# Two-layer transformer with soft and top-8 expert layers: another period table for layer 1, and the late wait written first

## Chip, cores and metric
One core of one Trainium2 chip runs the whole program. The metric is the time of one execution on the device, in microseconds (us); less is better. A program on one core has one span, and the engines named below are those of that core: PE (TensorE, matrix products), DVE (VectorE), ACT (ScalarE), POOL (GpSimd), SP (SyncE, which here issues most DMAs).

## Reference, cut to what matters
The input is 16 batches of 512 tokens with 128 features, f32. Each layer adds an attention and an expert network to the residual. Layer 0 normalizes, runs an attention with 16 heads of 8 and a rotary part, and a soft mixture of 8 experts with 64 slots each. Layer 1, in which most of the change lies, is:

```python
def _L1_attn_ref(x, w_kv_down, w_kv_up, w_q, w_out):
...
    latent_kv = x @ w_kv_down
    kv = latent_kv @ w_kv_up
    k, v = (kv[..., :HD], kv[..., HD:])
...
    att = jnp.einsum('bqhd,bkhd->bhqk', q, k) * scale
...
    att = jnp.where(causal, att, -jnp.inf)
    att = jax.nn.softmax(att, axis=-1)
    y = jnp.einsum('bhqk,bkhd->bqhd', att, v)
    y = y.reshape(Bx, Tx, HD)
    return y @ w_out

def _L1_ffn_ref(x, gate_w, expert_bias, w_gate, w_up, w_down, shared_gate_w, shared_up_w, shared_down_w):
...
    scores = jax.nn.sigmoid(gates.astype(jnp.float32))
    sel_scores = scores + expert_bias
    _, inds = jax.lax.top_k(sel_scores, K)
...
    selected = selected / selected.sum(axis=-1, keepdims=True)
    selected = selected * ROUTE_SCALE
...
    hg = jnp.einsum('bsd,eid->bsei', x, w_gate)
    hu = jnp.einsum('bsd,eid->bsei', x, w_up)
    h = jax.nn.silu(hg) * hu
    ye = jnp.einsum('bsei,edi->bsed', h, w_down)
    y = jnp.einsum('bsed,bse->bsd', ye, combine).astype(x.dtype)
    g = jnp.einsum('bsd,id->bsi', x, shared_gate_w)
    u = jnp.einsum('bsd,id->bsi', x, shared_up_w)
    y = y + jnp.einsum('bsi,di->bsd', jax.nn.silu(g) * u, shared_down_w)
    return y
...
xn = _layernorm(x, axis=-1)
x = x + _L0_attn_ref(xn, ...) + _L0_ffn_ref(xn, ...)
xn = _layernorm(x, axis=-1)
x = x + _L1_attn_ref(xn, ...) + _L1_ffn_ref(xn, ...)
```

There are 16 heads of 64 in layer 1, and K = 8 of E = 16 experts with 128 hidden values each are chosen for a token.

## The kernel before, in words
Layer 0 runs over all 16 batches, then layer 1. All 16 experts and the shared one are computed for every token; what the router did not choose gets weight 0.

**Products in halves.** A factor in f32 is split into a high and a low part in f16. A product is three matmuls into one PSUM bank: high x high, high x low, low x high (`split_product`, L1592 to L1594). So each intermediate leaves its bank twice: ACT writes the high part (q_hi, k_hi, v, lat_p and others, about L1318 to L1345), then DVE the low part (`low_part`, L1420: bank times a scale, less the high part), and after that the bank is free.

**Steps and the period table.** A batch of layer 1 is cut into steps: "load", "norm", "scale", "xnT" (normalize, transpose), "gate", "route", "cT" (router, weights, their transpose), "lat" (latent of keys and values), "qk" (per head group of 4 heads: two products of q, two of k), "v" (8 products), "max" (per head group five units of scores, whose row maxima DVE reduces in L1509 and L1513), "turn_max" (transpose of the maxima), "exp" (per pair of heads, 8 pairs, five units of scores; ACT takes their exponential twice, POOL makes the low part), "values" and "sums" (per pair: probabilities by v, and their row sums), "rec" (reciprocals of the sums of four pairs, L1525), "rec_out" and "rec_in" (these by DMA to DRAM and back, spread over the partitions), "divide" (L1533, two halves of 256 columns), "out" (the output product of four pairs, twice a batch), "gate_in" and "up_in" (two products per expert), "spread_in" (the routing weights of two experts from DRAM to all partitions, 512 KB), "hw" (the expert's hidden values in halves, L1358 and L1550), "down" (four chunks of experts, L1740), "outT", "res" (transpose, add the residual, store).

The table `ORDER1` (L953) lists the 195 steps of one period with the batch each belongs to, as an offset: ("divide", -1, 4) is pair 4 of the batch before. The program is this table repeated with the batch number counted up, from two batches before the first to two after the last, without what has no batch. Layer 0 has its own table, `ORDER0`. Every engine walks through the same list of steps and issues its own part of each, in that order, so the table fixes the order of the instructions on PE, ACT, DVE, POOL and SP alike. Nothing is reordered later: an instruction that waits holds all behind it on its engine. SP issues the DMAs of "load", "qk" (q and k stacked in SBUF), "turn_max" (the row of maxima into l_q_b), "cT" (weights to DRAM), "spread_in", "rec_out", "rec_in" and "res".

**Banks.** Layer 1 has four PSUM banks `ps_any` for everything but three things: the scores of "exp" have two banks `ps_exp`, "values" has `ps_out`, "sums" `ps_sum`. The class `Banks` (L107) walks through the table once and gives each product the bank of the four that was filled longest ago. Before its first matmul PE waits until the bank's last product was emptied (`bank`, which calls `emptied`), and a reader waits until its bank was filled (`full`, which calls `filling`). The probabilities have two slots of pairs, `p_in` three slots of units, `hid` five and `hw` eight slots of experts, `spread` three.

**Waits.** `eng.wait_ge(semaphore, count)` is put on the next instruction of the engine. An instruction carries one wait: where several are written ahead of it, the one written first stays on it, and the others become instructions of their own ahead of it.

**Shape of the array.** A matmul is named with rows x columns of the part of the array it uses: 128\*128 for products, 66\*128 for the second half of "exp", 64\*128 for "max", 128\*64 for "values", 128\*32 for "sums", 128\*16 for "turn_max".

## Time and profile before

| what | value |
|---|---|
| time, median of 3 runs | 2973.04 us (2971.9 to 2975.1) |
| the profiled execution's own time | 2973.48 us |
| its span | 2971.8 us |
| mean granted clock of PE | 0.989 of full speed |
| busy PE / DVE / ACT / POOL | 2792.8 / 2399.3 / 2074.8 / 1542.5 us |
| DMA | 298.15 MB, mean 100 GB/s |

The span goes from the first to the last instruction of the profiled execution; the rest of its own time lies around it. Matmuls overlap, and a matmul's row gives a duration in which the next one has already begun, so the distance between two starts says how long PE needs for one. A row of the timeline that ends in brackets gives the idle time of the engine ahead of it and what ended that. The granted clock is a share of 2.4 GHz. Layer 0 fills the first 1,150 us or so, layer 1 the rest.

### The profile page before, as it was taken

Reading aid. Unit: us, or ns where it says so; the run is one execution under the profiler, and the core shown is the slowest. Engines: PE = TensorE matmul, PEld = TensorE weight load, DVE = VectorE, ACT = ScalarE, POOL = GpSimd, SP = SyncE. Lnnn points to the kernel's source line nnn. Section 1 sums busy time; section 2 is a strip of 40 time slices with the busy share of each in tenths; the row PEclk is TensorE's granted clock in tenths of the full one; section 3 lists DMA queues with packets and bytes.
Section 4 is the critical chain, followed back from the end, with each engine's and each line's share of the span. In section 5 each row is a group of like instructions: output and inputs, shape, how many; then the busy total and the mean of one; then the engine's idle time right before and its main releaser. Section 6 shows DMA issues by size and latency. Waiting matters only on the chain.

```text
span 2971.8 us, 71998 instructions
## 1 busy us (share of the span) xinstructions
PE 2792.8 (94%) x27076; PEld 1596.6 (54%) x27076; DVE 2399.3 (81%) x4452; ACT 2074.8 (70%) x4411; POOL 1542.5 (52%) x1355
## 2 busy tenths in 40 slices
PE   5999999999999996999999999999999999999998
PEld 2555555555555553555555555555555555555554
DVE  6777777777777776888888888888888888888886
ACT  3777777677677765777777777777777777777764
POOL 2333333333333333665666666666666666666664
PEclk8999999999999998999999999999999999999999
DMA  4222222222222224454454464464454454454452
GB/s 126 59 55 55 66 67 56 68 58 57 55 58 61 55 55 128 109 142 113 115 145 118 110 148 115 111 150 113 111 149 113 112 149 112 112 146 115 111 147 69
DMA packets 272089, 298.15 MB, mean 100 GB/s; under 512 B 30848, under 2 KB 235648, under 8 KB 271488
## 3 DMA queue, kind: packets, MB, share of 16 engines
q1 hardware_dynamic: 247424, 274.70, 37.0%
q10 hardware_dynamic: 24320, 18.85, 2.0%
q8 instruction: 217, 3.56, 0.5%
q14 instruction: 128, 1.05, 0.1%
HBM read 141.39 MB, written 25.69 MB: 56 GB/s over the span
## 4 chain that ended last, share of the span: by engine, by line
PE 48%; DVE 6%; issue 3%; ACT 2%; DMA 1%; POOL 1%; SPq 0%; ACTq 0%; DVEq 0%; POOLq 0%
PE l_ps_out L1703 7%; PE l_ps_any L1592 5%; PE l_ps_any L1593 5%; PE l_ps_any L1594 5%; PE l_ps_exp L1684 4%; PE l_ps_any L1740 4%; PE l_ps_exp L1686 4%; PE l_ps_any L1749 4%; PE l_ps_any L1659 3%; PE l_ps_sum L1725 2%; PE l_ps_exp L1688 2%; PE l_ps_any L1664 1%; PE l_ps_any L1586 1%; DVE l_yT L1533 1%; DVE l_select L1431 1%
## 5 line engine op out<-in xcount | busy, mean ns | idle before, releaser
L1268 POOL TENSOR_TENSOR stage<-l_p_in,stage 128x512 f16<-128x512 f32 x640 | 759.3, 1198 | 405.5 <-ACT l_p_in L1381 404.5
L695 DVE TENSOR_REDUCE neg_max<-ps_any 128x1 f32<-128x384 f32 (+3 forms) x704 | 413.2, 635 | 118.3 <-PE ps_any L824 117.9
L1377 ACT ACTIVATE stage<-l_ps_exp 128x512 f16<-128x512 f32 x640 | 388.2, 607 | 157.3 <-PE l_ps_exp L1688 135.9
L1277 POOL TENSOR_TENSOR l_hid<-l_hid,l_spread 128x512 f32<-128x512 f32 x256 | 340.8, 1336 | 247.4 <-DVE l_hid L1546 211.8
L555 ACT ACTIVATE probs<-ps_exp 128x512 f32<-128x512 f32 x640 | 348.0, 605 | 95.4 <-PE ps_exp L839 90.6
L469 POOL TENSOR_SCALAR_AFFINE_SELECT probs<-probs 128x512 f32<-128x512 f32 x256 | 165.4, 664 | 441.6 <-ACT probs L555 441.6
L1381 ACT ACTIVATE l_p_in<-l_ps_exp 128x512 f32<-128x512 f32 x640 | 390.3, 610 | 0.0
L1513 DVE TENSOR_REDUCE l_neg_max<-l_ps_any 128x2 f32<-128x768 f32 (+2 forms) x384 | 310.9, 863 | 17.0 <-PE l_ps_any L1664 13.9
L822 PE MATMUL ps_any<-k_st,q_st 120*128 120x128 f16 (+3 forms) x1024 | 255.6, 305 | 70.8 <-DMA k_st<-stack_scratch 43.8
L1684 PE MATMUL l_ps_exp<-l_q_a,l_k_a 128*128 128x512 f16 (+3 forms) x1024 | 304.8, 300 | 3.2 <-DMA l_q_b<-l_max_row 1.6
L1686 PE MATMUL l_ps_exp<-l_q_b,l_k_b 66*128 66x512 f16 (+3 forms) x1024 | 295.5, 300 | 0.0
L1550 DVE TENSOR_TENSOR l_hw<-l_hid,l_hw 128x512 f16<-128x512 f32 x272 | 239.6, 886 | 6.2 <-ACT l_hw L1358 4.6
L1703 PE MATMUL l_ps_out<-stage,l_v 128*64 128x512 f16 (+3 forms) x3072 | 233.1, 301 | 0.0
L1387 ACT ACTIVATE l_hid<-l_ps_any 128x512 f32<-128x512 f32 x272 | 160.7, 614 | 102.8 <-PE l_ps_any L1594 98.2
L839 PE MATMUL ps_exp<-q_st,k_st 121*128 121x512 f16 (+3 forms) x1024 | 218.1, 302 | 4.6 <-DMA q_st<-max_row 2.4
L1688 PE MATMUL l_ps_exp<-l_mask_h,l_ident_h 128*128 128x128 bf16 x1024 | 212.5, 219 | 0.0
L1740 PE MATMUL l_ps_any<-l_hw,l_w_d 128*128 128x512 f16 x816 | 186.7, 379 | 16.3 <-DVE l_q_lo L1420 16.3
L824 PE MATMUL ps_any<-mask_h,ident_h 128*128 128x128 bf16 x1024 | 200.2, 221 | 0.0
L1358 ACT ACTIVATE l_hw<-l_hid 128x512 f16<-128x512 f32 x272 | 173.0, 642 | 33.3 <-POOL l_hid L1277 30.3
L1540 DVE SCALAR_TENSOR_TENSOR l_hid<-l_hid,l_ps_any 128x512 f32<-128x512 f32 x272 | 178.4, 678 | 21.2 <-ACT l_hid L1387 20.9
L1703 PEld LDWEIGHTS l_ps_out<-stage,l_v 128*64 128x64 f16 x3072 | 154.2, 110 | 76.1 <-issue 11.2
L459 POOL TENSOR_SCALAR disp_s<-disp_s,c_rec 128x512 f32<-128x512 f32 x64 | 105.4, 1652 | 167.7 <-DVE c_rec L704 167.7
(262 smaller groups left out, 6739.1 us busy)
## 6 DMA issues: line engine op xcount, KB each, us to landing
l_spread<-route_scratch SPq DMA_DIRECT2D x128, 512.0 KB, 5.0
l_q_a<-l_q_hi SPq DMA_DIRECT2D x256, 128.0 KB, 2.4
l_y_rec<-rec_scratch SPq DMA_DIRECT2D x128, 256.0 KB, 4.6
l_q_b<-l_q_lo SPq DMA_DIRECT2D x128, 128.0 KB, 2.4
l_k_a<-l_k_hi SPq DMA_DIRECT2D x128, 128.0 KB, 2.6
l_k_a<-l_k_lo SPq DMA_DIRECT2D x128, 128.0 KB, 2.8
l_k_b<-l_k_hi SPq DMA_DIRECT2D x128, 128.0 KB, 2.7
q_st<-rot_hi SPq DMA_DIRECT2D x64, 128.0 KB
```

What stands on the lines that cost most here:

```text
L555: nc.scalar.activation(probs[:, n % 2, u], ps_exp[:, (10 * g + u) % 3], ACT.Exp, scale=float(HD0 + DR) ** -0.5).then_inc(exp_done.sem, 1)
L695: nc.vector.tensor_reduce(neg_max[:, n % 2, heads[0]:heads[0] + k, t], src, AX.X, ALU.max, negate=True).then_inc(drained["dve"], 1)
L1268: nc.gpsimd.tensor_tensor(probs[:, n % 2, 1, u], p_in[:, m % P_SLOTS], probs[:, n % 2, 0, u], ALU.subtract).then_inc(p_lo_ok.sem, 1)
L1277: nc.gpsimd.tensor_tensor(at, at, spread[:, c % 3, n % SPREAD], ALU.mult).then_inc(weighted.sem, 1)
L1377: nc.scalar.activation(probs[:, n % 2, 0, u], bank, ACT.Exp, scale=float(HD1) ** -0.5).then_inc(exp_done.sem, 1)
L1381: nc.scalar.activation(p_in[:, m % P_SLOTS], bank, ACT.Exp, scale=float(HD1) ** -0.5).then_inc(p_ok.sem, 1)
L1513: ins = nc.vector.tensor_reduce(maxima[:, :, q, t], scores[:, :, c:c + (t + 1) * P], AX.X, ALU.max, negate=True)
L1684: pe.matmul(out, k_a[:, g % 2, h, k * P:k * P + P], q_a[:, g % 2, h, k * P:T], start=True, stop=False)
L1686: pe.matmul(out, k_b[0:K_B, g % 2, h, k * P:k * P + P], q_b[0:K_B, g % 2, h, k * P:T], start=False, stop=False)
L1688: ins = pe.matmul(out[:, 0:P], ident_h[:], mask_h[:], start=False, stop=True)
L1703: ins = pe.matmul(ps_out[HD1 * r:HD1 * r + HD1, k * P:T], v[:, k, cv, h * HD1:h * HD1 + HD1], probs[:, n % 2, cp, u, c:c + T - k * P], sta ...
L1740: ins = pe.matmul(out, w_d[:, cw, e], hw[:, k % HW_SLOTS, cx], start=(e == todo[0] and cw + cx == 0), stop=(e == todo[-1] and cw == 1))
```

## The change
Two things are changed.

1. The table `ORDER1` is another one. It has the same steps of each kind per period; "load" stands one batch further ahead (offset 2), and some steps of the next batch have come into the table of the period, others of the batch before have left it. `ORDER0` stays.
2. Where several waits are written ahead of an instruction, their order is changed. In "exp" ACT waits first for the scores, then for "values" and "sums" of the pair before. `low_part` (DVE) waits first for the high part, and for its bank not at all, since the high part's ACT instruction has waited for that; so do "slots", "low_q", "low_k", "dispatch", "combine" and one "logits" of layer 0. "hidden" of layer 0 waits first for its bank. "values" and "sums" (PE) wait first for the low parts of the probabilities. "logits" of layer 0 waits for xfT for n = 0 alone.

Two lines are added in layer 1 and one in layer 0, so L1420 before is L1423 now, L1533 is L1536, L1592 is L1595, L1740 is L1743. The diff, with the table cut to its first lines:

```diff
@@ exp of layer 1, ACT (the same in layer 0, there with pv_done alone)
                     p, u = PAIRS * b + n, step[3]
+                    act.wait_ge(exp_full.sem, exp_full.at(p, u + 1))
                     if u == 0 and p >= 2:
                         act.wait_ge(pv_done.sem, pv_done.at(p - 1, 0))
                         act.wait_ge(summed.sem, summed.at(p - 1, 0))
-                    act.wait_ge(exp_full.sem, exp_full.at(p, u + 1))
@@ low_part of layer 1, DVE
-                bank = full(dve, name)
                 dve.wait_ge(sem.sem, count)
+                bank = ps_any[:, banks.at[name]]
@@ slots of layer 0, DVE (so too dispatch, combine, low_q, low_k; logits on ACT)
-                    bank = full(dve, f"slots{b}")
+                    bank = ps_any[:, banks.at[f"slots{b}"]]
                     dve.wait_ge(slots_hi.sem, slots_hi.at(b, 1))
@@ hidden of layer 0, ACT
+                    bank = full(act, f"hidden{b}_{n}")
                     if b and n == 0:
                         filling(act, f"expert_out{b - 1}")
-                    bank = full(act, f"hidden{b}_{n}")
@@ logits_s and logits_c of layer 0, PE
-                    emptied(pe, f"xfT{b}")
+                    if n == 0:
+                        emptied(pe, f"xfT{b}")
@@ values of layer 1, PE
                     p = PAIRS * b + n
+                    pe.wait_ge(p_lo_ok.sem, p_lo_ok.at(p, 5))
                     if p:
                         pe.wait_ge(y_ok.sem, y_ok.at(p, 0))
                     if n % SET == 0:
                         emptied(pe, f"v{b}_{TB - 1}{n // SET}")
-                    pe.wait_ge(p_lo_ok.sem, p_lo_ok.at(p, 5))
@@ sums of layer 1, PE
+                    pe.wait_ge(p_lo_ok.sem, p_lo_ok.at(p, 5))
                     if j == 0 and p >= SET:
                         pe.wait_ge(rec_ok.sem, rec_ok.at(p // SET, 0))
-                    pe.wait_ge(p_lo_ok.sem, p_lo_ok.at(p, 5))
@@ the table
 ORDER1 = (
-    ("max", 0, 0, 2), ("max", 0, 0, 3), ("values", -1, 5), ("max", 0, 0, 4), ("divide", -1, 1), ("hw", -1, 15),
...
+    ("exp", -1, 7, 2), ("qk", 0, 1, 0), ("exp", -1, 7, 3), ("outT", -2), ("rec_in", -1, 1), ("gate_in", 0, 1),
...
```

What the table moves is shown at three places, in a batch in the middle of layer 1.

**First place, PE, "down" of chunk 0.** Before, it stands behind one gate product, one k product and a unit of "exp", all behind the two q products of head group 2 (w_q is q's weight, w_kvu that of keys and values, w_g the experts' gate weight):

```order
L1592 MATMUL l_ps_any<-l_xn_p,l_w_g 128x512 [waits l1_drained_dve]
L1593 MATMUL l_ps_any<-l_xn_p,l_w_g 128x512
L1594 MATMUL l_ps_any<-l_xn_p,l_w_g 128x512
L1592 MATMUL l_ps_any<-l_lat_p,l_w_kvu 128x512 [waits l1_drained_dve]
L1593 MATMUL l_ps_any<-l_lat_p,l_w_kvu 128x512
L1594 MATMUL l_ps_any<-l_lat_p,l_w_kvu 128x512
L1684 MATMUL l_ps_exp<-l_q_a,l_k_a 128x512 [waits l1_p_ok]
L1686 MATMUL l_ps_exp<-l_q_b,l_k_b 128x512
L1688 MATMUL l_ps_exp<-l_mask_h,l_ident_h 128x128
L1740 MATMUL l_ps_any<-l_hw,l_w_d 128x512 [waits l1_hw_ok,l1_drained_dve]
L1740 MATMUL l_ps_any<-l_hw,l_w_d 128x512 x2
```

Now, in the same batch, after the last units of "exp" of a pair:

```order
L1687 MATMUL l_ps_exp<-l_q_a,l_k_a 128x256
L1689 MATMUL l_ps_exp<-l_q_b,l_k_b 128x256
L1691 MATMUL l_ps_exp<-l_mask_h,l_ident_h 128x128
L1595 MATMUL l_ps_any<-l_xn_p,l_w_g 128x512 [waits l1_drained_dve]
L1596 MATMUL l_ps_any<-l_xn_p,l_w_g 128x512
L1597 MATMUL l_ps_any<-l_xn_p,l_w_g 128x512
L1743 MATMUL l_ps_any<-l_hw,l_w_d 128x512 [waits l1_hw_ok,l1_drained_dve]
L1743 MATMUL l_ps_any<-l_hw,l_w_d 128x512 x2
...
L1595 MATMUL l_ps_any<-l_xn_p,l_w_q 128x512 [waits l1_drained_dve]
L1596 MATMUL l_ps_any<-l_xn_p,l_w_q 128x512
L1597 MATMUL l_ps_any<-l_xn_p,l_w_q 128x512
```

"down" has moved ahead of the q and k products of head group 2; a gate product alone stands between it and "exp", and the first q product comes after it.

**Second place, DVE, "divide" of pairs 4 and 5 of the batch before** (two rows each, l_yT<-l_yT,l_y_rec). Before, each stands between low parts of q and k of head group 2:

```order
L1420 SCALAR_TENSOR_TENSOR l_v<-l_ps_any,l_v 128x512 [waits l1_v_hi_ok,l1_filled]
L1533 TENSOR_TENSOR l_yT<-l_yT,l_y_rec 128x2x128 [waits l1_rec_in,l1_y_ok]
L1533 TENSOR_TENSOR l_yT<-l_yT,l_y_rec 128x256
L1420 SCALAR_TENSOR_TENSOR l_q_lo<-l_ps_any,l_q_hi 128x512 [waits l1_hi_ok,l1_filled]
L1550 TENSOR_TENSOR l_hw<-l_hid,l_hw 128x512 [waits l1_hw_hi]
L1533 TENSOR_TENSOR l_yT<-l_yT,l_y_rec 128x2x128 [waits l1_rec_in,l1_y_ok]
L1533 TENSOR_TENSOR l_yT<-l_yT,l_y_rec 128x256
L1420 SCALAR_TENSOR_TENSOR l_k_lo<-l_ps_any,l_k_hi 128x512 [waits l1_hi_ok,l1_filled]
L1540 SCALAR_TENSOR_TENSOR l_hid<-l_hid,l_ps_any 128x512 [waits l1_filled,l1_tanh_ok]
L1420 SCALAR_TENSOR_TENSOR l_k_lo<-l_ps_any,l_k_hi 128x512 [waits l1_hi_ok,l1_filled]
L1550 TENSOR_TENSOR l_hw<-l_hid,l_hw 128x512 [waits l1_hw_hi]
L1557 TENSOR_SCALAR l_acc<-l_ps_any 128x512 [waits l1_filled]
```

Now (the first "divide" here is that of pair 3):

```order
L1536 TENSOR_TENSOR l_yT<-l_yT,l_y_rec 128x2x128 [waits l1_rec_in,l1_y_ok]
L1536 TENSOR_TENSOR l_yT<-l_yT,l_y_rec 128x256
L1549 TENSOR_TENSOR l_hid<-l_ps_any,l_hid 128x512 [waits l1_filled,l1_drained_dve] x2
L1564 SCALAR_TENSOR_TENSOR l_acc<-l_ps_any,l_acc 128x512 [waits l1_drained_dve,l1_filled]
L1512 TENSOR_REDUCE l_neg_max<-l_ps_any 128x2x2 [waits l1_filled]
L1516 TENSOR_REDUCE l_neg_max<-l_ps_any 128x2 [waits l1_filled]
L1516 TENSOR_REDUCE l_neg_max<-l_ps_any 128x2
L1536 TENSOR_TENSOR l_yT<-l_yT,l_y_rec 128x2x128 [waits l1_rec_in,l1_y_ok]
L1536 TENSOR_TENSOR l_yT<-l_yT,l_y_rec 128x256
L1553 TENSOR_TENSOR l_hw<-l_hid,l_hw 128x512 [waits l1_hw_hi]
L1536 TENSOR_TENSOR l_yT<-l_yT,l_y_rec 128x2x128 [waits l1_rec_in,l1_y_ok]
```

All three have come close together, ahead of the first low part of head group 2, with two reductions of "max" (L1512, L1516) and an add to the accumulator (L1564) between pair 3 and pair 4.

**Third place, PE, the transpose of the maxima of the next batch's head group 0** (L1669 before, L1672 now). Before, units of "exp" of the pair before follow it:

```order
L1725 MATMUL l_ps_sum<-stage,l_ones_in 32x256 x2
L1725 MATMUL l_ps_sum<-stage,l_ones_in 32x128 x6
L1669 MATMUL l_ps_any<-ident,l_neg_max 16x128 [waits l1_drained_dve]
L1684 MATMUL l_ps_exp<-l_q_a,l_k_a 128x384 [waits l1_p_ok]
L1686 MATMUL l_ps_exp<-l_q_b,l_k_b 128x384
L1688 MATMUL l_ps_exp<-l_mask_h,l_ident_h 128x128
L1684 MATMUL l_ps_exp<-l_q_a,l_k_a 128x128
```

Now six products follow, and then the first "exp" that reads the row of maxima (it waits for l1_row_in):

```order
L1672 MATMUL l_ps_any<-ident,l_neg_max 16x128 [waits l1_drained_dve]
L1595 MATMUL l_ps_any<-l_xn_p,l_w_q 128x512 [waits l1_drained_dve]
L1596 MATMUL l_ps_any<-l_xn_p,l_w_q 128x512
...
L1595 MATMUL l_ps_any<-l_lat_p,l_w_kvu 128x512 [waits l1_drained_dve]
L1596 MATMUL l_ps_any<-l_lat_p,l_w_kvu 128x512
...
L1595 MATMUL l_ps_any<-l_xn_p,l_w_u 128x512 [waits l1_drained_dve]
...
L1595 MATMUL l_ps_any<-l_xn_p,l_w_u 128x512 [waits l1_drained_act]
...
L1595 MATMUL l_ps_any<-l_lat_p,l_w_kvu 128x512 [waits l1_drained_dve]
...
L1595 MATMUL l_ps_any<-l_xn_p,l_w_g 128x512 [waits l1_drained_dve]
...
L1687 MATMUL l_ps_exp<-l_q_a,l_k_a 128x512 [waits l1_p_ok,l1_stacked,l1_row_in]
```

Before, twelve products and the rest of the exp units stood between the two; now it is six products alone.

## Rows read from the trace of the kernel before

**Rows 1.** The page, part 1: busy time, share of the span, instructions
```profile
PE 2792.8 (94%) x27076; PEld 1596.6 (54%) x27076; DVE 2399.3 (81%) x4452; ACT 2074.8 (70%) x4411; POOL 1542.5 (52%) x1355
```
**Rows 2.** Window of one period: us, PE, PEld, DVE, ACT, POOL busy, PEclk, DMA, GB/s
```profile
1650.20:1761.20 111.00, 109.28 (x1074) 60.91 (x1072) 96.50 (x162) 80.12 (x159) 70.41 (x58) 1.00 0.52 125
```
**Rows 3.** Instructions of L1557: ns min/median/max, first and last start
```profile
L1557 DVE TENSOR_SCALAR l_acc<-l_ps_any x16: 676/678/692, 1215.7 to 2882.4; 128x512 f32<-128x512 f32 x16
```
**Rows 4.** Waits of PE, 1300 to 2850: us in total, times, longest us
```profile
PE l_ps_any L1740 <- DVE l_q_lo L1420: 15.5, 14, 1.5
PE l_ps_any L1592 <- DVE l_lat_p L1420: 5.3, 14, 0.4
PE l_ps_exp L1684 <- DMA l_q_b<-l_max_row: 1.6, 3, 0.8
```
**Rows 5.** Timeline, PE, 2000 to 2012: start us, us, engine, line, operation, count
```profile
2003.04 0.22 PE L1688 MATMUL l_ps_exp<-l_mask_h,l_ident_h 128*128 128x128 bf16 x1
2003.10 0.38 PE L1592 MATMUL l_ps_any<-l_xn_p,l_w_u 128*128 128x512 f16 x1
...
2010.73 0.22 PE L1688 MATMUL l_ps_exp<-l_mask_h,l_ident_h 128*128 128x128 bf16 x1
2010.88 1.33 PE L1703 MATMUL l_ps_out<-stage,l_v 128*64 128x512 f16 x12
```
**Rows 6.** Timeline, PE: round two transposes of maxima and a k product
```profile
1756.33 0.28 PE L1669 MATMUL l_ps_any<-ident,l_neg_max 128*16 128x128 f32 x1
...
1760.89 0.38 PE L1684 MATMUL l_ps_exp<-l_q_a,l_k_a 128*128 128x512 f16 x1
...
2006.77 0.38 PE L1594 MATMUL l_ps_any<-l_lat_p,l_w_kvu 128*128 128x512 f16 x1
```
**Rows 7.** Timeline, ACT and DVE, 2004 to 2008: high and low parts
```profile
2004.67 0.60 ACT L1336 ACTIVATE l_q_hi<-l_ps_any 128x512 f16<-128x512 f32 x1 [0.29 <-PE l_ps_any L1594]
2005.37 0.69 DVE L1420 SCALAR_TENSOR_TENSOR l_q_lo<-l_ps_any,l_q_hi 128x512 f16<-128x512 f32 x1 [0.67 <-ACT l_q_hi L1336]
...
2007.19 0.60 ACT L1336 ACTIVATE l_k_hi<-l_ps_any 128x512 f16<-128x512 f32 x1
```
**Rows 8.** Tile slotsT, layer 0, 150 to 1070: who waited for it, us, times
```profile
  PEld ps_any L763: 4.9, 13
```
**Rows 9.** Timeline, DVE and PE, 1762 to 1767: "divide" and "down"
```profile
1762.13 2.41 DVE L1533 TENSOR_TENSOR l_yT<-l_yT,l_y_rec 128x256 f32<-128x256 f32 x2
...
1763.76 0.22 PE L1688 MATMUL l_ps_exp<-l_mask_h,l_ident_h 128*128 128x128 bf16 x1
1765.19 1.04 PE L1740 MATMUL l_ps_any<-l_hw,l_w_d 128*128 128x512 f16 x4 [1.22 <-DVE l_q_lo L1420]
...
1766.02 0.75 DVE L1533 TENSOR_TENSOR l_yT<-l_yT,l_y_rec 128x256 f32<-128x256 f32 x2
```
**Rows 10.** Timeline, DVE: first instruction of "route" and the one behind it
```profile
1698.08 0.21 DVE L1429 TENSOR_SCALAR l_score<-l_th 128x64 f32<-128x64 f32 x1
...
1703.41 0.68 DVE L1420 SCALAR_TENSOR_TENSOR l_q_lo<-l_ps_any,l_q_hi 128x512 f16<-128x512 f32 x1
```
**Rows 11.** DMA issues, 1300 to 2850: count, KB each, median us to landing
```profile
l_spread<-route_scratch SPq DMA_DIRECT2D x111, 512.0 KB, 5.0
...
l_y_rec<-rec_scratch SPq DMA_DIRECT2D x112, 256.0 KB, 4.6
...
l_q_b<-l_max_row SPq DMA_DIRECT2D x56, 4.0 KB, 3.0
route_scratch<-l_weightT SPq DMA_DIRECT2D x14, 32.0 KB, 1.9
```
**Rows 12.** Timeline, POOL, 1717 to 1736: the batch's first weighting
```profile
1727.90 1.27 POOL L1277 TENSOR_TENSOR l_hid<-l_hid,l_spread 128x512 f32<-128x512 f32 x1 [2.79 <-DMA l_spread<-route_scratch]
```
**Rows 13.** Groups by line, 1500 to 2700: busy us, mean ns, idle before
```profile
L1550 DVE TENSOR_TENSOR l_hw<-l_hid,l_hw 128x512 f16<-128x512 f32 x183 | 159.6, 877 | 1.2
L1533 DVE TENSOR_TENSOR l_yT<-l_yT,l_y_rec 128x256 f32<-128x256 f32 x172 | 90.2, 565 | 0.6 <-DMA l_y_rec<-rec_scratch 0.6
```

76 lines of the change are left out of this document (39 added, 37 removed).

## Prediction

> **What bounds the kernel now.** I read the page first: PE is busy for 94% of the span, DVE 81%, ACT 70%, POOL 52% [rows 1]. Then one period of layer 1 (one batch), the part whose order changes: PE works 109.28 of 111.00 us, DVE 96.50 beside it, at a granted clock of 1.00 [rows 2]. The first "down" of a batch starts the accumulator, from 1215.7 to 2882.4 us over 16 batches: (2882.4 - 1215.7) / 15 = 111.11 us a period [rows 3]. So PE is the bound, and time can go in two ways: less work on PE, or shorter waits of PE. The list of waits shows what PE stood still for in 14 periods: 15.5 us (1.11 a period) before "down" for l_q_lo on DVE, 5.3 us (0.38) before a product for l_lat_p, 1.6 us before exp for a DMA [rows 4]. Idle is counted from the end of the last matmul; start to start a wait costs 0.16 us more, since a matmul of 0.22 us is followed by the next after 0.06 us [rows 5]. The two big waits thus cost 1.27 and 0.54, together 1.8 us a period.
>
> **Changes of the array's shape.** After an exp's last 128-column matmul (128*128) the next one starts 0.06 us later if it has the same shape (2003.04, 2003.10), but 0.15 us later if it is the 128*64 of "values" (2010.73, 2010.88) [rows 5]. A change costs 0.09 us. Counted in the table ("max" is 64*128, "values" 128*64, "sums" 128*32, all else full width), a period has 49 changes before and 44 after; the whole program, its ends included, 782 and 703. The 79 that go are worth 79 x 0.093 = 7.3 us (0.08 and 0.10 by the rounding: 6 to 8), all on PE; nothing hides them.
> The Trainium skill, "TensorEngine Tiling (Array Packing)", Key Properties, says that changing the tiling mode drains the engine, and "TensorE: Matmul & The Clock Gate", Part 2, puts the drain at about 128 cycles; by these pages 79 changes would be an estimated 4.2 us at 2.4 GHz, and the sum 3 us higher. The rows have 0.09 for one, and I take them.
>
> **Waits written in another order.** The first wait that is written rides on the instruction, the others become instructions of their own ahead of it. ACT's l_k_hi, which waits for its bank alone, starts at 2007.19, as its matmul ends (2006.77 + 0.38 = 2007.15): 0.04 us. On DVE l_q_lo, whose late wait was written second, starts at 2005.37, 0.10 us after its l_q_hi (2004.67 + 0.60) [rows 6, 7]. So 0.06 us or a little more a time, where the wait was really late. In layer 1 this touches the first exp of a pair and DVE's low parts; PE's two big waits there end on a DVE queue that was busy before the job, so the cover is that queue, and without it the price is at most two such jobs, 0.1 us a period. I take nothing. In layer 0 one such place is on PE's way: PE waited for DVE's slotsT 13 times in 13 batches [rows 8], and the first "hidden" behind it has its bank wait moved to the front too. That is 16 x 2 x 0.06 = 1.9 us. Layer 0's order and banks stay. The repeated waits that go (a low part's bank, which the high part has waited for; xfT for n > 0) lie in queues that run ahead: nothing, and nothing to lose. On PE, "values" and "sums" now carry the wait for the low parts and check the others first, which are long met.
>
> **The waits that the new order removes.** "down" of chunk 0 takes the bank of the second q product of head group 2. DVE's queue shows why it is late: two halves of "divide" take 2.41 us (1762.13), l_q_lo stands behind them, and PE, which waits for it, starts at 1765.19 where it would have started 0.06 us after 1763.76 [rows 9]. In the new order (the first place shown) "down" stands before these products and takes a bank of "max", left 2.15 us of PE's work earlier, with one reduction of 1.2 us to wait for. The 1.27 us go. The second wait comes from "route", 5.33 us of DVE in one piece (1698.08 to 1703.41) [rows 10], behind which lat's low part stood; now lat stands before it. Behind route now stand two k products; the first of their banks is wanted again 3.05 us of PE's work later, about when DVE has it free: 0 to 0.5 us, I take 0.1. Net 1.7 us a period.
>
> **What is late next.** Four places are tighter; PE's work between steps is counted from the order at 0.65 us a product of three matmuls (four of "down" take 1.04 us [rows 9], one 0.38, so 0.22 from start to start).
> (a) The row of maxima of head group 0: transpose, ACT, a DMA of SP (median 3.0 us [rows 11]), exp. Now six products lie between, 6 x 0.65 + 0.11 = 4.0 us (third place), where there were 12. Head group 1 has 1756.33 to 1760.89, 4.56 us [rows 6], and the only waits of this kind, 1.6 us in 14 periods [rows 4]. With 0.56 us less: 0.4 us a period (0 to 1.5).
> (b) POOL's first weighting of a batch waits for the spread table; it already idles 2.79 us for it, to 1727.90, with no harm [rows 12]. From cT: 1.1 us to the end of ACT's copy, 1.9 to DRAM, 5.0 back [rows 11], 1.27 for the weighting and three low parts at 1.2, 12.9 us, until "sums" of pair 7 has what it needs; PE gets there after 15.4. With two spreads and a load in flight the landing grows: 0.2 us (0 to 1.2).
> (c) After the fourth unit of "max" of head group 3 DVE has two reductions (2.4), two reciprocals (1.8), three jobs and a v low part (3.0), 7.2 us, and that v's bank is wanted 7.1 us after DVE could begin: 0.4 us (0 to 1.5).
> (d) "divide" of pairs 4 and 5 follows that of pair 3 after 8 us of PE's work instead of 18 (second place). Between them lies the trip of the reciprocals, two issues by SP and 4.6 us to landing [rows 11]: 0.3 us (0 to 2).
> Together 1.3 us, with 0.1 for the rest of the ring 1.4 against 1.7 removed: 0.3 x 16 = 5 us.
>
> **Sum.** -7.3 - 1.9 - 5 = -14 us against the profiled execution's 2973.5 us (span 2971.8), which lies 0.4 us above the median of the runs, 2973.0. Start and tail have the same steps, the tail the same trips of the reciprocals: nothing, 3 us either way. **2959 us.** Bounds: every new wait at zero gives -7.3 - 1.9 - 29 = 2935. The upper ends add to 6.2 us a period, but a wait at one place gives the queues time at the next; half of it, 3.1 against 1.8, gives -9 + 21, 2985.
>
> **Rivals.**
> A. The new order has next to no waits. For it: DVE has 14.5 us free in a period. Against: (a), (c) and (d) are each at the edge. -9 - 27: 2937 us. Chance 0.21.
> B. The waits come back in full size elsewhere. The change then doesn't do what a new order is for, since DVE has 96.5 us of work in 111 and four banks to hand over, whatever the order [rows 2]; the shapes remain, less what is added: 2970 us (2964 to 2976). Chance 0.14.
> C. Slower, by (d). If the reciprocals land later than DVE arrives, DVE stands still with all behind it, and the add of "out", four jobs on, holds the bank that the next "max" wants 1.3 us after "out": each us of lateness is one of PE, 16 in all. For it: I put DVE at divide 4 some 14 us into the period, and the landing at 13.3 to 15. Against: "out" itself is 3.4 us of PE's work and covers the first of it. From 2.3 us of new waits a period it is slower than before; at 3.3 it is 2989 us. Chance 0.21.
> D. DVE's jobs with two operands in SBUF meet POOL's more often. l_hw has a mean of 877 ns and a half of divide 565 [rows 13], where l_q_lo has 680 for as many columns and an undisturbed half 0.37 [rows 9]: 17 x 0.2 + 16 x 0.2 = 6.6 us a period already. The new order sets hw and divide in groups; 2 us more of it would give PE perhaps 0.8: 2972 us. Chance 0.06.
> The Trainium skill, "SBUF — State Buffer", on the shared port pair, says that such an operation and a GpSimd one that reads SBUF exclude each other for the whole instruction.
>
> **How the numbers follow.** The forecast's own case (2949 to 2967) has 0.38. A measurement can tell about 0.2%, 6 us. Faster by more: 0.38 + 0.21 + 0.06 of B = 0.65. Within: 0.08 of B + 0.06 of D = 0.14. Slower: C, 0.21. The range goes from A's low end, 2935, to 2988, and leaves out half of C and a little of A.
>
> **What would show it.** A period of 110.2 us between first "down"s; L1740's idle for l_q_lo and L1592's for l_lat_p gone; PE's wait for max_row before exp under 0.5 us a period, and for POOL before "sums" under 0.4. It is wrong if PE's idle before "max" for l_acc, or DVE's before l_yT for a DMA, passes 1 us a period, if the first low part of v becomes a wait of over 1 us, or if layer 0's period moves by more than 0.3 us.

## The result and the profile after

The changed kernel takes 2979.15 us (median of 16 runs, 2972.46 to 2985.15), the kernel before 2972.38 us (16 runs, 2970.78 to 2975.10). The ratio is 1.0024 with an interval of 1.0016 to 1.0032: 0.24% slower, some 7 us, where 14 us faster was forecast. The runs of the changed kernel also lie further apart, 12.7 us against 4.3.

That small number is the sum of two large ones. The page's first part and the two steps that occur once in a batch show them. First the busy times, which answer to [rows 1]:

```profile
PE 2792.6 (94%) x27076; PEld 1599.7 (54%) x27076; DVE 2451.9 (82%) x4452; ACT 2075.0 (70%) x4411; POOL 1583.8 (53%) x1355
```

PE has as much to do as before; DVE is busy 52.6 us longer with the same 4452 instructions. Now one instruction of layer 0 (ACT's slotsT, L540 before, L541 after) and the first "down" of layer 1 (L1560, before in [rows 3]): duration in ns, then first and last start. Of before:

```profile
L540 ACT ACTIVATE slotsT<-ps_any x16: 597/597/598, 74.1 to 1100.9; 128x512 f16<-128x512 f32 x16
```

and of after:

```profile
L541 ACT ACTIVATE slotsT<-ps_any x16: 597/597/597, 72.8 to 1084.4; 128x512 f16<-128x512 f32 x16
L1560 DVE TENSOR_SCALAR l_acc<-l_ps_any x16: 677/678/679, 1187.7 to 2887.4; 128x512 f32<-128x512 f32 x16
```

By (last - first start) / 15, layer 0 went from 68.45 to 67.44 us a batch, though its table is the same, and layer 1 from 111.11 to 113.31. The last slotsT comes 16.5 us earlier, "down" runs through its 15 periods in 1699.7 us instead of 1666.7, 33 us more.

What PE waited for in layer 1, 1300 to 2850 us, the same view as [rows 4] (us in total, times, longest us):

```profile
PE l_ps_any L1595 <- DVE l_v L1423: 23.1, 27, 1.3
PE l_ps_any L1662 <- DVE l_acc L1569: 22.2, 13, 2.0
PE l_ps_any L1752 <- DVE l_yT L1536: 4.2, 14, 0.3
PE l_ps_any L1595 <- DVE l_acc L1560: 1.0, 3, 0.3
PE l_ps_any L1662 <- DVE l_neg_max L1512: 0.2, 1, 0.2
```

The two waits of before, for l_q_lo and l_lat_p, are gone, as the change means it. In their place stand two others, for l_v and for l_acc, and together they are twice as long: 50.7 us of idle in 58 waits against 23.9 in 35. With the 0.16 us that each wait costs from start to start beyond its idle time, that is (50.7 + 9.3) / 14 = 4.3 us a batch against 2.1.

### Where layer 1's new wait comes from

The list of DVE's waits of the changed kernel begins with a DMA, of which the kernel before has 0.6 us in all between 1500 and 2700 [rows 13]:

```profile
DVE l_yT L1536 <- DMA l_y_rec<-rec_scratch: 47.3, 16, 4.3
```

One batch of it, on DVE: the reciprocals, "divide" of pair 3 and "divide" of pair 4 (start us, us):

```profile
2062.10 1.76 DVE L1528 RECIPROCAL l_rec<-l_ps_sum 128x128 f32<-128x128 f32 x2
...
2067.31 2.11 DVE L1536 TENSOR_TENSOR l_yT<-l_yT,l_y_rec 128x256 f32<-128x256 f32 x2
...
2077.71 0.91 DVE L1536 TENSOR_TENSOR l_yT<-l_yT,l_y_rec 128x256 f32<-128x256 f32 x2 [3.85 <-DMA l_y_rec<-rec_scratch]
```

The DMA queue of SP in the same stretch:

```profile
2061.59 0.53 SPq L1221 DMA_DIRECT2D l_spread<-route_scratch  x1
2062.16 0.59 SPq L1201 DMA_DIRECT2D l_k_a<-l_k_hi  x1
...
2065.44 0.61 SPq L1201 DMA_DIRECT2D l_k_b<-l_k_hi  x1
2066.16 0.52 SPq L1221 DMA_DIRECT2D l_spread<-route_scratch  x1
2066.80 0.38 SPq L1229 DMA_DIRECT2D rec_scratch<-l_rec  x1
2071.85 9.30 SPq L1238 DMA_DIRECT2D l_y_rec<-rec_scratch  x4
```

And PE, which stands still for the add of "out" behind "divide":

```profile
2081.24 0.34 PE L1662 MATMUL l_ps_any<-l_k_hi,l_q_hi 64*128 64x384 f16 x2 [1.74 <-DVE l_acc L1569]
2081.46 0.23 PE L1662 MATMUL l_ps_any<-l_k_hi,l_q_hi 64*128 64x128 f16 x2
2081.68 1.82 PE L1706 MATMUL l_ps_out<-stage,l_v 128*64 128x512 f16 x24
```

The reciprocals are ready at 2063.86. SP is then in the middle of six stack DMAs of k and a spread of 512 KB, so rec_out goes out at 2066.80, 2.9 us late (median of such places 3.3 us; before 0.1). It lands 5.0 us later (median 4.7; before 1.7), 0.36 us after the spread that was issued 0.64 us ahead of it. So it is in nearly every batch: in the changed kernel a spread is under way at 31 of the 32 issues of rec_out, and 30 of these land 0.3 to 0.5 us after the spread does; in the kernel before none of the 32 meets a spread. rec_in follows at 2071.85 and lands at about 2077.6. DVE has stood still since 2073.9. This is the mechanism of rival C, and it is what (d) put at 0.3 us.

### The profile page after: what moved, and what is told of

Same layout as the page of the kernel before. It is cut to its first block, busy times and chain, and to the rows that moved or that the text cites. A ratio compares the mean times of both kernels' runs of the same rounds, so it can differ in the third digit from the quotient of the medians.

```text
span 2982.3 us, 71219 instructions
## 1 busy us (share of the span) xinstructions
PE 2792.6 (94%) x27076; PEld 1599.7 (54%) x27076; DVE 2451.9 (82%) x4452; ACT 2075.0 (70%) x4411; POOL 1583.8 (53%) x1355
## 4 chain that ended last, share of the span: by engine, by line
PE 32%; DVE 12%; issue 6%; DMA 6%; SPq 3%; POOL 2%; ACT 1%; ACTq 0%; POOLq 0%; DVEq 0%
PE l_ps_out L1706 5%; PE l_ps_any L1595 4%; PE l_ps_any L1743 4%; DVE l_yT L1536 4%; PE l_ps_any L1597 3%; PE l_ps_any L1596 3%; DMA l_y_rec<-rec_scratch 3%; PE l_ps_exp L1687 3%; PE l_ps_exp L1689 3%; PE l_ps_any L1662 3%; DMA rec_scratch<-l_rec 2%; SPq L1201 2%; DVE l_hw L1553 2%; PE l_ps_sum L1728 2%; DVE l_hid L1543 1%
## 5 line engine op out<-in xcount | busy, mean ns | idle before, releaser
L1271 POOL TENSOR_TENSOR stage<-l_p_in,stage 128x512 f16<-128x512 f32 x640 | 785.8, 1243 | 372.3 <-ACT l_p_in L1384 371.4
L1280 POOL TENSOR_TENSOR l_hid<-l_hid,l_spread 128x512 f32<-128x512 f32 x256 | 348.4, 1366 | 271.0 <-DVE l_hid L1549 249.2
L1516 DVE TENSOR_REDUCE l_neg_max<-l_ps_any 128x2 f32<-128x768 f32 (+2 forms) x384 | 315.1, 863 | 40.4 <-PE l_ps_any L1667 37.2
L1536 DVE TENSOR_TENSOR l_yT<-l_yT,l_y_rec 128x256 f32<-128x256 f32 x256 | 203.1, 838 | 61.7 <-DMA l_y_rec<-rec_scratch 61.4
L1553 DVE TENSOR_TENSOR l_hw<-l_hid,l_hw 128x512 f16<-128x512 f32 x272 | 245.7, 912 | 2.3 <-ACT l_hw L1361 1.9
L1549 DVE TENSOR_TENSOR l_hid<-l_ps_any,l_hid 128x512 f32<-128x512 f32 x272 | 180.9, 679 | 12.8 <-PE l_ps_any L1597 12.3
L1743 PE MATMUL l_ps_any<-l_hw,l_w_d 128*128 128x512 f16 x816 | 188.0, 382 | 0.0
```

The source lines that it names most:

```text
L1271: nc.gpsimd.tensor_tensor(probs[:, n % 2, 1, u], p_in[:, m % P_SLOTS], probs[:, n % 2, 0, u], ALU.subtract).then_inc(p_lo_ok.sem, 1)
L1280: nc.gpsimd.tensor_tensor(at, at, spread[:, c % 3, n % SPREAD], ALU.mult).then_inc(weighted.sem, 1)
L1516: ins = nc.vector.tensor_reduce(maxima[:, :, q, t], scores[:, :, c:c + (t + 1) * P], AX.X, ALU.max, negate=True)
L1536: ins = nc.vector.tensor_tensor(part, part, y_rec[:, f, n % 2].rearrange("p (c q) -> p c q", q=P), ALU.mult)
L1743: ins = pe.matmul(out, w_d[:, cw, e], hw[:, k % HW_SLOTS, cx], start=(e == todo[0] and cw + cx == 0), stop=(e == todo[-1] and cw == 1))
```

## The experiments

All runs, in the order in which they were made. The medians of e1 to e12 are of 4 to 6 executions each, and each ratio is to executions of the kernel before made along with them (medians 2969.4 to 2972.0). "Layer 0" and "layer 1" are us a batch of the profiled execution, (last - first start) / 15 of slotsT and of the first "down".

| run | what it is | median us | ratio to before (interval) | layer 0 | layer 1 |
|---|---|---|---|---|---|
| before | | 2972.4 | 1 | 68.45 | 111.11 |
| after | | 2979.2 | 1.0024 (1.0016 to 1.0032) | 67.44 | 113.31 |
| e1_waits | old table, new waits | 2947.8 | 0.9921 (0.9908 to 0.9933) | 67.25 | 110.99 |
| e2_table | new table, old waits | 3005.4 | 1.0113 (1.0099 to 1.0126) | 68.47 | 113.37 |
| e3_table_loads | before, two edits on ACT | 2946.9 | 0.9923 (0.9909 to 0.9936) | 66.93 | 111.12 |
| e4_rec_first | after, rec and rec_out earlier | 2958.3 | 0.9954 (0.9941 to 0.9966) | 67.29 | 111.73 |
| e5_spread_behind | after, a spread behind rec_out | 2961.6 | 0.9966 (0.9953 to 0.9978) | 67.17 | 111.86 |
| e6_divide_behind_v | e4, divide 6 later | 2947.4 | 0.9919 (0.9904 to 0.9933) | 66.97 | 111.21 |
| e7_divide_behind_q | e1, divide 4 later | 2946.2 | 0.9913 (0.9898 to 0.9929) | 66.95 | 110.83 |
| e8_both_new_table | e5, divide 6 later | 2953.3 | 0.9935 (0.9920 to 0.9950) | 66.88 | 111.41 |
| e9_rec_out_first | e8, rec_out alone earlier | 2951.0 | 0.9935 (0.9920 to 0.9950) | 66.95 | 111.29 |
| e10_divide_behind_hw | e9, divide 6 later still | 2939.8 | 0.9894 (0.9880 to 0.9909) | 67.11 | 110.75 |
| e11_hidden_alone | before, one of e3's edits | 2955.9 | 0.9949 (0.9932 to 0.9966) | 67.45 | 111.11 |
| e12_divide_3_earlier | e10, divide 3 earlier | 2948.5 | 0.9924 (0.9910 to 0.9937) | 66.91 | 111.31 |

### The two halves apart: e1_waits and e2_table

e1 is the changed kernel with `ORDER1` of before, e2 the kernel before with `ORDER1` of after; no other line differs.

> The table of before with every wait in its new order. Theory: in layer 0 the load of ACT's function table for Gelu (L572) and for Exp (L527) carried the bank's wait and so began only when PE was done; with the new order it begins early, and a batch of layer 0 takes 66.5 us instead of 68.15. If that is all of it, and layer 1's period stays at 111.1 us, the time is 2973 - 16 x 1.65 = 2947 us (2943 to 2955). Rival, my own prediction: waits cost 0.06 us each and the new order gives 2 us, 2971 us. If layer 1 gains or loses by the waits, its period moves from 111.1 us; I expect less than 0.2 us.

> The new table with every wait as before. Theory: the gain of the change is layer 0's waits alone and the loss is layer 1's table alone, so this one lacks the gain: layer 0 at 68.15 us a batch, layer 1 at 113.5 us, 2979 + 22 = 3001 us (2993 to 3008). Rival: the new order of waits is what slows layer 1 (values and sums wait first for the low parts, exp first for its scores): then layer 1's period falls towards 110.2 us here and the time is about 2960 us.

Measured: 2947.8 and 3005.4 us. The waits alone are worth -24 us, the table alone +33. Both together should give 2972.4 - 24.6 + 33 = 2981; it is 2979.2. The two add up to within 2 us, and the rival that the new order of waits slows layer 1 falls: layer 1 is at 113.37 us with the old waits too, and at 110.99 with the new ones on the old table.

### Why layer 0 is faster: e3_table_loads and e11_hidden_alone

The waits of PE in layer 0, 150 to 1070 us, before:

```profile
PE ps_any L822 <- ACT disp_s L527: 8.6, 14, 0.6
...
PE ps_any L828 <- ACT hT L572: 7.2, 13, 0.6
PE ps_any L822 <- ACT max_row L545: 3.4, 14, 0.2
```

All three are on ACT, and none is in the same list of after. They are 19.2 us of idle in 41 waits, 25.8 us with 0.16 us for each. ACT's timeline of one batch, before:

```profile
348.39 0.60 ACT L562 ACTIVATE y_un<-ps_out 128x512 f32<-128x512 f32 x1
350.27 1.28 ACT L572 ACT_TABLE_LOAD   x1 [1.28 <-PE ps_any L765]
351.56 3.39 ACT L572 ACTIVATE hT<-ps_any,b 128x64 f32<-128x64 f32 x16
...
359.15 1.28 ACT L527 ACT_TABLE_LOAD   x1 [0.90 <-PE ps_any L765]
360.45 0.69 ACT L527 ACTIVATE disp_s<-ps_any,c_neg 128x512 f32<-128x512 f32 x1
```

and after:

```profile
340.66 0.60 ACT L563 ACTIVATE y_un<-ps_out 128x512 f32<-128x512 f32 x1
341.27 1.28 ACT L573 ACT_TABLE_LOAD   x1
342.57 3.38 ACT L573 ACTIVATE hT<-ps_any,b 128x64 f32<-128x64 f32 x16
...
349.78 1.28 ACT L528 ACT_TABLE_LOAD   x1
351.08 0.69 ACT L528 ACTIVATE disp_s<-ps_any,c_neg 128x512 f32<-128x512 f32 x1
```

ACT changes its function table twice a batch, for Gelu and back for Exp, 1.28 us each. No line of the kernel says so; the load has the line of the activation it serves. The trace's records of ACT show what held it. The load waits for nothing itself. The activation has the wait that was written first, and the wait for the bank, written second, is an instruction of its own, which ends at 350.24 and 359.13 us. It stands ahead of the load, and the load starts right behind it, at 350.27 and 359.15. So for "hidden" ACT idled 1.28 us until PE had filled the bank, and only then loaded the table, and 0.90 us for Exp. In the changed kernel the bank's wait of "hidden" is on the activation, behind the load, and that of Exp is gone; the load runs at once, beside PE's work. e3 makes these two edits alone, on the kernel before:

```diff
                 if name in ("soft_s", "soft_c"):
-                    nc.scalar.activation(w[:, n], full(act, f"logits{name[4:]}{b}_{n}"), ACT.Exp, ...
+                    logits = ps_any[:, banks.at[f"logits{name[4:]}{b}_{n}"]]
+                    nc.scalar.activation(w[:, n], logits, ACT.Exp, ...
                 if name == "hidden":
+                    bank = full(act, f"hidden{b}_{n}")
                     if b and n == 0:
                         filling(act, f"expert_out{b - 1}")
-                    bank = full(act, f"hidden{b}_{n}")
```

> Before, with two edits in layer 0 on ACT alone: hidden waits for its bank first, and the logits' bank wait ahead of Exp goes. Theory: these two free the table loads and hold nearly all of the gain of the new waits, 1.3 to 1.7 us a batch: 2946 to 2953 us, within 5 us of all the new waits on the old table. Rival: the gain comes from the 17 wait instructions that are gone per batch on ACT and DVE; two of these would give at most an eighth of it, 2970 us.

Measured 2946.9 us, as much as all the new waits (2947.8). The groups of the two loads over the program (busy us, mean ns, idle before) are, before:

```profile
L572 ACT ACT_TABLE_LOAD x16 | 20.5, 1283 | 20.6 <-PE ps_any L765 20.6
L527 ACT ACT_TABLE_LOAD x16 | 20.5, 1283 | 14.3 <-PE ps_any L765 14.3
```

and in e3:

```profile
L573 ACT ACT_TABLE_LOAD x16 | 20.5, 1283 | 1.7 <-PE ps_any L766 1.4
L528 ACT ACT_TABLE_LOAD x16 | 20.5, 1283 | 0.3
```

The other new waits, on DVE, on PE and in layer 1, give nothing that can be told: the rival of the 17 fewer wait instructions falls. e11 takes the edit on "hidden" alone (the last three lines of the diff).

> Before, with one edit: hidden of layer 0 waits for its bank first, so that the wait no longer stands on the load of Gelu's table (1.28 us, L572). Theory: the load starts when ACT is free and PE's idle before L828 for hT (0.57 us a batch) and before L822 for max_row (0.24) goes; with the 0.16 us between end and start of matmuls counted, 0.8 to 1.0 us a batch: 2972 - 14 = 2958 us (2954 to 2962), and the other edit (the logits' bank wait on Exp's table load) has the rest, 0.6 to 0.8 us a batch. Rival: the two loads are in one chain, and freeing one alone gives either nothing (2970) or all (2948).

Measured 2955.9 us, 14 to 16 us of the 25. PE's waits for hT and max_row are gone, the one for disp_s is still 8.7 us in 14 batches. So neither load hides the other; each is worth its own waits. (Layer 0's periods of 66.9 to 67.4 us in the runs that have both edits differ for another reason, told under "Clock" below.)

### Why layer 1 is slower: e4_rec_first, e5_spread_behind, e9_rec_out_first

These runs change when rec_out goes out. In e4 the reciprocals go earlier, on DVE and SP. In e5 only the spread goes behind them. e8 is e5 with divide 6 moved (below), and e9 is e8 with rec_out alone earlier, a step of SP:

```diff
 after:  ("hw", 0, 0), ("qk", 0, 1, 3), ("gate_in", 0, 4), ("exp", 0, 0, 0), ("spread_in", 0, 3), ("rec", -1, 1), ("rec_out", -1, 1),
+e4:     ("hw", 0, 0), ("rec", -1, 1), ("rec_out", -1, 1), ("qk", 0, 1, 3), ("gate_in", 0, 4), ("exp", 0, 0, 0), ("spread_in", 0, 3),
+e5:     ("hw", 0, 0), ("qk", 0, 1, 3), ("gate_in", 0, 4), ("exp", 0, 0, 0), ("rec", -1, 1), ("rec_out", -1, 1), ("spread_in", 0, 3),
+e9:     ("hw", 0, 0), ("rec_out", -1, 1), ("qk", 0, 1, 3), ("gate_in", 0, 4), ("exp", 0, 0, 0), ("spread_in", 0, 3), ("rec", -1, 1),
```

> The changed kernel with rec and rec_out of the second half of the heads moved ahead of the last k product of head group 1, so that the reciprocals leave before SP's six stack DMAs and before the spread of 512 KB (spread_in 3 now stands behind them). Theory: DVE's idle of 2.5 to 4.3 us a batch before l_yT for l_y_rec falls below 1 us, PE's idle before max for l_acc (22 us in 14 batches) to under 0.3 us a batch, and the dips of the granted clock behind it go: 1.5 to 2.2 us a batch, 2979 - 30 = 2949 us (2942 to 2962). Rival 1: DVE is too full for it, the waits of PE move to the first low part of v or to out, and less than 0.5 us a batch is gained: 2972 us or more. Rival 2: the two reciprocals of 0.9 us that now stand earlier hold the banks of the q and k products: a new wait of PE there of over 0.5 us a batch.

> The changed kernel with one step put later: spread_in 3 (512 KB) stands behind rec and rec_out, no longer ahead of them; rec stays where it is. Theory: what made the reciprocals late was mostly the spread issued 0.6 us ahead of them (their trip to DRAM took 3.7 to 5.5 us, 1.8 in the kernel before); now rec_out goes out 0.6 us earlier and lands after 2 us, rec_in starts 3.5 us earlier, DVE's idle before l_yT falls from 3.4 us a batch to under 0.8, PE's for l_acc to under 0.3. Without the earlier reciprocals there is no new wait for l_k_lo either: layer 1 at 111.4 us a batch (111.0 to 112.0), 2950 us (2944 to 2960). Rival: it was SP's queue of six stack DMAs ahead of rec_out (2.9 us after the reciprocals' end) that counted; then the spread moves only 0.6 us and the collision is merely turned round, DVE still waits over 2 us a batch, and the time stays above 2968 us.

> The changed kernel with rec_out (a step of SP alone) moved ahead of the last k product of head group 1, so ahead of SP's six stack DMAs and of the spread; the reciprocals on DVE stay where they are, and divide of pair 6 stands behind the low part of v 2,1. Theory: the trip is late by both, issue queue (2.9 us) and collision (3.2 us); with both gone rec_out is issued 0.1 us after the reciprocals and DVE's idle for l_y_rec is under 0.3 us a batch, PE has neither the wait for l_acc nor the one for l_k_lo that the earlier reciprocals brought. Layer 1 at 110.7 us a batch (110.4 to 111.1), 2947 - 13 = 2934 us (2929 to 2942). Rival: SP, standing still for the reciprocals, brings the stack DMAs late and exp waits for them; or DVE's queue, which no longer idles, gives the wait at another bank: 2944 us or more.

For the trip of the second half's reciprocals the traces give these medians, and beside them DVE's idle for l_y_rec and PE's for l_acc between 1300 and 2850 us:

| run | reciprocals' end to rec_out's issue | issue to landing | DVE for l_y_rec | PE for l_acc (L1569) |
|---|---|---|---|---|
| before | 0.1 us | 1.7 us | under 1 us | none |
| after | 3.3 | 4.7 | 47.3 | 22.2 |
| e4_rec_first | 0.1 | 3.6 | 7.4 | 1.0 |
| e5_spread_behind | 2.6 | 3.8 | 22.8 | 9.8 |
| e9_rec_out_first | 0.1 | 2.0 | 21.0 | 11.2 |

e4 shows the theory right: with the reciprocals in time PE's wait for l_acc falls from 22.2 to 1.0 us, layer 1 gains 1.6 us a batch, and 21 us of the program go, of the 30 forecast. Its second rival came true as well, for a smaller amount: a wait of 10.0 us in 14 batches for l_k_lo, behind the reciprocals that now stand earlier on DVE. e5 falls between theory and rival (2961.6 us, forecast under 2960 or over 2968): half of DVE's idle went, with 0.7 us less lag and a landing 0.9 us faster, and half stayed. In e9 rec_out leaves at once, when the spread ahead of it has only about 1.5 us to go, and lands in 2.0 us, yet DVE still idles 21 us, and the expectation of 2934 us was missed by 17. Its SP queue says why:

```profile
2045.74 0.33 SPq L1229 DMA_DIRECT2D rec_scratch<-l_rec  x1
...
2051.25 1.24 SPq L1238 DMA_DIRECT2D l_y_rec<-rec_scratch  x2
```

rec_out had landed at 2047.7, but rec_in went out at 2051.25, 0.03 us after the end of "divide" of pair 3. There is one table l_y_rec for two pairs, and rec_in waits until the last divide has read it (`y_div` in SP's "rec_in"). So the chain is: divide 3, rec_in, 6.6 us to landing (2057.9), divide 4, and the new table leaves only six other instructions of DVE, 4.5 us, between the two divides. A second table of reciprocals should cut this chain; that was not tried. e12 moves divide 3 three jobs ahead instead (behind hw 1):

> The run with divide of pair 6 behind hw 11, and divide of pair 3 three jobs of DVE earlier, behind hw 1. There is one table of reciprocals in SBUF for two pairs, so rec_in of pairs 4 and 5 waits for the end of divide 3, whatever rec_out does: in the last two runs its DMAs were issued 0.03 us after that end and landed 5.3 to 6.5 us later, and DVE, four jobs on, idled 1.0 to 2.2 us. Theory: with divide 3 some 2 us earlier this idle falls from 1.6 to under 0.4 us a batch and PE's for l_acc from 0.85 to under 0.2; layer 1 at 110.2 us a batch, 2940 - 12 = 2928 us (2923 to 2934). Rival: divide 3, 2.1 us under POOL's work, now stands ahead of three jobs whose banks PE wants, and gives a new wait of as much there: 2936 us or more.

DVE's idle for l_y_rec fell to 3.0 us and PE's for l_acc to 0.5, as the theory has it. The time rose to 2948.5 us from e10's 2939.8, where 2928 was forecast. Its rival has come true; of PE's two largest waits the first is new:

```profile
PE l_ps_any L1595 <- DVE l_hid L1549: 19.6, 14, 1.4
PE l_ps_any L1752 <- DVE l_yT L1536: 6.9, 12, 0.6
```

### The other new wait: e6_divide_behind_v, e7_divide_behind_q, e8_both_new_table, e10_divide_behind_hw

The wait for l_v stands behind "divide" of pair 6. DVE and POOL there, in the changed kernel:

```profile
2012.23 2.81 DVE L1536 TENSOR_TENSOR l_yT<-l_yT,l_y_rec 128x256 f32<-128x256 f32 x2
2014.96 0.68 DVE L1423 SCALAR_TENSOR_TENSOR l_v<-l_ps_any,l_v 128x512 f16<-128x512 f32 x1
```

```profile
2011.79 1.66 POOL L1280 TENSOR_TENSOR l_hid<-l_hid,l_spread 128x512 f32<-128x512 f32 x1 [0.71 <-DVE l_hid L1549]
2013.40 1.34 POOL L1271 TENSOR_TENSOR stage<-l_p_in,stage 128x512 f16<-128x512 f32 x1
```

The two halves take 1.5 and 1.4 us instead of the 0.37 each of [rows 9] (0.75 us for two). They end 0.3 us after POOL's two instructions (2013.45 and 2014.74). So it is with nearly every half longer than 0.7 us: 47 of the 48 before and 115 of the 131 after (of 256 each) end 0.28 to 0.29 us after a POOL instruction does; the mean of a half between 1500 and 2700 us rose from 565 ns [rows 13] to 854:

```profile
L1536 DVE TENSOR_TENSOR l_yT<-l_yT,l_y_rec 128x256 f32<-128x256 f32 x168 | 136.0, 854 | 40.1 <-DMA l_y_rec<-rec_scratch 40.0
```

Over the whole program the 256 halves took 69.6 us more (214.6 against 145.0), which is more than DVE's extra 52.6 us; "route" and others took less. POOL's instructions took 41.3 us more in all. The Trainium skill, "SBUF — State Buffer", on the shared port pair, says that a DVE operation with both inputs in SBUF and a GpSimd operation that reads SBUF exclude each other for the whole instruction; the ends of the long halves agree with that. The runs move these divides behind the low part that PE wants, each against the run named in the table:

```diff
+e6, e8:  ("v", 0, 2, 1), ("divide", -1, 6),
-         ("divide", -1, 6), ("v", 0, 2, 1),
+e7:      ("spread_in", 0, 5), ("qk", 0, 2, 1), ("divide", -1, 4), ("hw", 0, 5),
-         ("divide", -1, 4), ("spread_in", 0, 5), ("qk", 0, 2, 1), ("hw", 0, 5),
+e10:     ("v", 0, 2, 1), ("exp", 0, 4, 2), ("gate_in", 0, 13), ("gate_in", 0, 14), ("hw", 0, 11), ("divide", -1, 6),
-         ("v", 0, 2, 1), ("divide", -1, 6), ("exp", 0, 4, 2), ("gate_in", 0, 13), ("gate_in", 0, 14), ("hw", 0, 11),
```

> The run with rec first, and beside it divide of pair 6 behind the low part of v 2,1 instead of ahead of it. Theory: that divide takes 2.8 us instead of 0.8, because POOL works at the same time, and the low part behind it is what PE waited for 1.3 us a batch before a gate product; now this wait is under 0.2 us. With 0.16 us of start to start that is 1.3 us a batch, 2958 - 20 = 2938 us (2933 to 2945). Rival: the queue of DVE stays as long, the wait comes back within the next 15 us at another bank, and less than 0.4 us a batch is gained: 2952 us or more.

> The old table with the new waits, and divide of pair 4 behind the low part of the second q product of head group 2 instead of ahead of it. Theory: PE's largest wait of the kernel before, 1.07 us of idle a batch before down for l_q_lo, is this divide at 2.4 us under POOL's work ahead of the low part; with it behind, the wait falls below 0.1 us: 1.1 to 1.2 us a batch, 2948 - 18 = 2930 us (2925 to 2937), without a new table. Rival: the k products' low parts behind the divide become late instead and half or more comes back: 2939 us or more.

> The changed kernel with spread_in 3 behind rec_out and divide of pair 6 behind the low part of v 2,1. By the theory both waits of PE go without a new one: layer 1 at 110.2 us a batch (109.9 to 110.7), what its five fewer changes of shape were worth among it; 2979 - 16 x 3.3 = 2926 us (2921 to 2938). If it does not get below the old table with the new waits (2948 us) the new table gives nothing even when its two new waits are gone.

> The run before this, and divide of pair 6 another three jobs of DVE later, behind hw 11. In the kernel with rec first and the divide behind v, 9.0 us of PE's idle for l_hid and 6.5 us for l_v in 14 batches were left. Theory: both are this divide's 2.8 us under POOL's work ahead of a low part that is wanted soon; three jobs later it stands before nothing that is wanted soon: PE's idle for l_hid and l_v together under 0.3 us a batch, 0.8 us a batch less than without this move, 2934 - 13 = 2921 us. Rival: DVE is behind by a fixed amount and the wait moves on once more: less than 0.3 us a batch, within 5 us of the run before this.

e6: 2947.4 us, 11 us gained where 20 were forecast; the 18 us of waits for the first of the two l_v went, and 9.0 us came back for l_hid behind the same divide. e7: 2946.2 us, against 2930 forecast. The largest wait of the kernel before, for l_q_lo (14.9 us in e1), is gone, and in the old table 11.4 us for l_k_lo stand in its place; nothing that can be told was gained. This is what the rivals of both runs say. e8: 2953.3 us against 2926; of the changed kernel's two waits neither went, l_v's shrank to 6.3 us and l_acc's to 12.4, and 8.9 us for l_hid are new. So it does not get below the old table with the new waits (2947.8). e10: 2939.8 us against 2921, 11 us less than e9, where its own step was forecast at 13: three jobs later the divide no longer delays l_hid, whose 9.0 us are gone. 5.4 us for l_v stay, and the wait for l_yT grew from 3.8 to 7.4. It is the fastest version of the study, 1.1% faster than before (0.9894, 0.9880 to 0.9909); some 25 of the 33 us are the table loads.

## Why the prediction was wrong, point by point

**The waits removed from layer 1** ("The 1.27 us go"; lat now 0.1): right. Neither stands in the list of after.

**Shapes** (-7.3 us): no run tested them alone, but the sums agree. e10 has the new table's 44 changes, e1 the old one's 49. e1's idle is 22.8 us in 32 waits, e10's 24.9 in 42, so with 0.16 us each 1.99 and 2.26 us a batch. 110.99 + 0.27 - 5 x 0.093 = 110.80 us; measured 110.75. The Trainium skill's drain of about 128 cycles at the end of a matmul ("TensorE: Matmul & The Clock Gate", Part 2), an estimated 0.05 us, would, if it is what a change costs, give 111.0 us instead; the sum is too coarse to rule it out.

**The order of waits in layer 0** ("16 x 2 x 0.06 = 1.9 us"): the step that was most wrong. They are worth 25 us (e1, e3). The price of 0.06 us was for a wait that becomes an instruction of its own right ahead of the work; I did not ask what stands between the two. For "hidden" and the router's Exp a table load of 1.28 us stands there. The program's lines don't show it, and the groups and the timeline of before do, with "1.28 <-PE" behind it. That layer 0's period moves by more than 0.3 us was named as a sign that the forecast is wrong, and it moved by 1.0. The other three signs came too: PE's idle for l_acc before "max" and DVE's for a DMA before l_yT passed 1 us a batch (1.6 and 3.4), and the first low part of v became a wait of 1.3 us.

**(a)** the row of maxima, 0.4 us a batch: it cost nothing, and the 1.6 us of before went with it. **(b)** the spread, 0.2: no wait at "sums" in the list of after.

**(c)** v behind the reciprocals, 0.4 us (0 to 1.5): right in place, wrong in size. The v of the second half waits 1.3 us a batch, at the upper bound with 0.16 us more from start to start, and another v adds 0.3 to 0.6. The term put three jobs and the low part of v together at 3.0 us; "divide" of pair 6, which stands right ahead of that low part, alone took 2.8 us, and e6, with it behind, has 18 us less of this wait.

**(d)** "two issues by SP and 4.6 us to landing: 0.3 us (0 to 2)": the term that gave the sign. It measured 3.4 us of DVE's idle and 1.6 us of PE's a batch, inside its bounds and over five times its value. With the reciprocals out in time (e4) 21 us of the program go, and the change would have been a gain. The trip was taken with the durations of before. In the new place rec_out waits 3.3 us in SP's queue, lands in 4.7 us instead of 1.7 beside a spread, and rec_in waits for divide 3 as well (e9, e12). Every DMA issue on the queue and every reuse of the tile should have been written down, as the place itself was.

**A term that is missing**: the wait for l_yT before "out" (L1752), 4.2 us of idle in 14 waits, 0.46 us a batch with 0.16 us for each. Before it is not in the list.

**D** (DVE against POOL): had a chance of 0.06 and 2 us of DVE's time a batch. It came beside C, and at twice its size on DVE: the halves of "divide" alone grew by 16 x 0.29 = 4.6 us a batch. What PE lost by it is shown at one place, "divide" of pair 6 (e6); elsewhere it was not separated.

**Clock**: not in the prediction. In the changed kernel's profile the granted clock falls to the lower level four times in layer 1 between 1700 and 2800 us, where before it stays at 1.00. One of these (columns as in [rows 2]), and PE there:

```profile
1737.00:1741.00 4.00, 2.26 (x25) 1.18 (x23) 4.00 (x8) 1.57 (x3) 1.10 (x2) 1.00 0.02 8
1741.00:1745.00 4.00, 4.00 (x41) 2.32 (x36) 1.36 (x3) 0.70 (x2) 0.38 (x1) 0.57 0.47 127
```

```profile
1740.55 0.34 PE L1662 MATMUL l_ps_any<-l_k_hi,l_q_hi 64*128 64x384 f16 x2 [1.74 <-DVE l_acc L1569]
1740.99 3.21 PE L1706 MATMUL l_ps_out<-stage,l_v 128*64 128x512 f16 x24
```

The same "values" took 1.82 us at 2081.68. At the lower level, 1.2 GHz for some microseconds, it loses 1.4 us, right behind the idle for l_acc. With about 1.7 us for each of four such places in 14 batches this is 0.5 us a batch, and the account of layer 1 closes: 4.28 - 2.11 = 2.2 us more waits, less 0.47 for shapes, plus 0.5, gives 2.2; measured 113.31 - 111.11 = 2.20. e2, the same table with the old waits, had no such fall and 55.8 us of idle in 68 waits, 4.76 us a batch: 4.76 - 2.11 - 0.47 = 2.18, measured 2.26. All four falls came right behind an idle of 1.7 to 2.0 us for l_acc. Why not behind the others (2081 had 1.74 us, and one of 2.02 us at 1627 had none behind it either) stays open, and no run tested it alone. Layer 0 has such falls too, in different number from run to run: between 150 and 1050 us none before, four in the changed kernel (67.44 us a batch), two in e1 and e4 (67.25, 67.29), none in e8 and e9 (66.88, 66.95). At up to 1.7 us each in 15 periods they would be most of the difference. They may also be part of why the changed kernel's executions lie far apart; that is not shown.

**The whole.** Rival C, at 0.21, had the mechanism that made the table slower, and too small a size: at its 3.3 us of new waits a batch (the sum had 1.4) layer 1 would take 1.0 us a batch more, (3.3 - 1.8) - 0.47. It took 2.2 us more. Of the 4.28 us of waits 1.7 are for l_acc, which is C's and (d)'s, and 2.0 for two l_v, the longer of which is (c)'s. The table alone costs 33 us (e2), where C's 2989 us has some 17 for it. The measured time of 2979.15 lies within the forecast's range only because layer 0's gain, taken as 1.9 us, paid for 25 of it. So the range holds the time by luck, by two errors that cancel, and the direction was wrong: (c) and (d) cost more than the table's gain.

## What to carry to other kernels

When waits are put in another order, look for what stands between a wait that is an instruction of its own and the work that it guards: a function table load put ahead of an activation stands there, so a late wait written second holds the load too. A row "ACT_TABLE_LOAD ... [1.28 <-PE ...]" in the timeline can be time to be had with one line moved. When a round trip over DRAM gets less cover, write its whole chain for the new place (end of the producer, the issues ahead of it on the queue, the transfers under way beside it, who still reads the tile that it fills), since durations of the old place don't hold. With DVE at 87 to 90% in layer 1 and four banks a removed wait tended to come back in part or in full at the next bank (e6, e7, e12): say for each moved job of 2 to 3 us which low part stands behind it.

## What the runs showed of the hardware

A table load on ACT took 1.28 us, twice a batch. It stood between the wait written second, an instruction of its own, and the activation, which carried the wait written first. A DMA of 128 KB from the reciprocals to DRAM took 1.7 us in the median (1.7 to 3.2) when no 512 KB spread was under way, in 169 cases of all runs. Issued behind a spread that had 1.4 us or more to go, it landed 0.4 us after the spread in the median of 248 cases, and in 234 of them within 0.6 us: 4.7 us from issue to landing in the changed kernel, 2.0 us in e9. And a DVE operation of 0.37 us with both operands in SBUF took up to 1.5 us, in 115 of the 131 long cases to 0.28 or 0.29 us past the end of POOL's instruction.
